# Keys turned by VectorE and transfers instead of TensorE, SyncE's program laid out by steps, and two small operations moved to ScalarE

## What is computed

```
Q, K = (x @ Wq.T), (x @ Wk.T)              # 16 heads of 64
V    = x @ Wv.T                            # 16 heads of 16
g    = -exp(A_log) * softplus(x @ Wdt.T + dt_bias);  cg = cumsum(g)
Lam  = softplus(Lp * (x @ Wdl.T))          # 12 levels for each head
W    = (Q K^T / 8) * exp(cg_t - cg_s) * Lam[t, level(t xor s)]    (s <= t)
a    = layernorm((W V) @ Wout.T + x) * ln_g + ln_b
x    = layernorm(x + a)                    # the "outer norm"
for two steps t:  f, i, u = sigmoid, sigmoid, tanh of (x_t @ w + c @ u + b);  c = f*c + i*u
x    = layernorm(x + tanh(x @ wo.T + c @ uo.T + bo))
```

## Time and profile before

| | |
|---|---|
| time, median of 3 runs | 681.56 us (680.77 to 683.13) |
| time of the profiled execution | 682.09 us |
| its span (first to last instruction) | 680.5 us |
| granted TensorE clock, mean | 0.982 of full speed |
| DMA engines, mean busy share | 25.6% for the kernel's own transfers |
| DMA packets under 512 bytes | 39664 of 91987 |

### The profile page before, as it was taken

How to read it: one execution, slowest core, us unless ns; L and a number is a source line. 1 busy time by engine, 2 the same in 40 slices (tenths; PEclk the granted TensorE clock), 3 DMA queues, 4 the chain that set the end, 5 groups by cost and what they waited for, 6 DMA issues and landing times.

```text
span 680.5 us, 22147 instructions
## 1 busy us (share of the span) xinstructions
PE 657.1 (97%) x9114; PEld 594.8 (87%) x9114; DVE 486.8 (72%) x1100; ACT 337.0 (50%) x755; POOL 353.9 (52%) x475
## 2 busy tenths in 40 slices
PE   9989999999999999999999999999689999999994
PEld 7889999999999999899999999999588788888894
DVE  2864887879787978676797879787749565555556
ACT  4565454445545454545445454545253434555555
POOL 1716555646474655656464646556365435444435
PEclk9999999999999999999999999999888999999997
DMA  8122131312222141213132322313126503140002
GB/s 306 30 56 60 48 75 41 76 46 71 64 53 76 42 94 42 64 41 76 43 74 55 60 73 45 87 50 82 53 71 122 103 9 62 47 86 31 32 33 92
DMA packets 91987, 45.47 MB, mean 67 GB/s; under 512 B 39664, under 2 KB 90480, under 8 KB 91888
## 3 DMA queue, kind: packets, MB, share of 16 engines
q1 hardware_dynamic: 91888, 44.06, 25.6%
HBM read 34.60 MB, written 9.44 MB: 65 GB/s over the span
## 4 chain that ended last, share of the span: by engine, by line
PE 86%; DVE 5%; ACT 2%; POOL 2%; DMA 1%; SPq 1%; issue 1%; DVEq 0%; ACTq 0%; POOLq 0%
PE bank L437 64%; PE bank L461 5%; PE bank L528 5%; PE bank L440 5%; PE bank L493 4%; PE bank L557 4%; DMA xt<-in_wffn 1%; ACT t L791 1%; SPq L371 1%; DVE t L1028 1%; DVE t L1031 1%; POOL t L1415 1%; SPq L348 0%; POOL yL L1415 0%; DVE W L1028 0%
## 5 line engine op out<-in xcount | busy, mean ns | idle before, releaser
L437 PE MATMUL bank<-xH,wH 128*128 128x256 f32 x480 | 144.3, 301 | 1.2 <-ACT KT L791 0.9
L437 PE MATMUL bank<-xL,wH 128*128 128x256 f32 x480 | 135.0, 281 | 0.0
L437 PE MATMUL bank<-xH,wL 128*128 128x256 f32 x480 | 134.6, 280 | 0.0
L1028 DVE TENSOR_TENSOR W<-bank,E 128x512 f32<-128x512 f32 x128 | 82.0, 685 | 25.7 <-PE bank L437 25.4
L437 PEld LDWEIGHTS bank<-xH,wH 128*128 128x128 f32 x480 | 90.4, 188 | 7.8 <-issue 7.3
L437 PEld LDWEIGHTS bank<-xL,wH 128*128 128x128 f32 x480 | 90.5, 189 | 0.4
L437 PEld LDWEIGHTS bank<-xH,wL 128*128 128x128 f32 x480 | 90.5, 188 | 0.0
L791 ACT ACTIVATE E<-bank 128x512 f32<-128x512 f32 x128 | 66.1, 602 | 48.8 <-PE bank L461 48.8
L791 ACT ACTIVATE QT<-bank 128x512 f32<-128x512 f32 x64 | 38.2, 597 | 98.5 <-PE bank L437 98.5
L437 PE MATMUL bank<-QT,KT 64*128 64x128 f32 x1024 | 65.8, 278 | 0.0
L437 PEld LDWEIGHTS bank<-QT,KT 64*128 64x128 f32 x1024 | 59.6, 188 | 4.5 <-issue 0.5
(11 more groups left out here) (151 smaller groups left out, 1657.9 us busy)
## 6 DMA issues: line engine op xcount, KB each, us to landing
cB<-scr SPq DMA_DIRECT2D x240, 64.0 KB, 3.0
xt<-in_xT SPq DMA_DIRECT2D x16, 256.0 KB, 3.1
xs<-in_x SPq DMA_DIRECT2D x16, 256.0 KB, 3.1
xscr<-tx SPq DMA_DIRECT2D x32, 128.0 KB, 2.0
yT<-xscr SPq DMA_DIRECT2D x64, 64.0 KB, 2.4
out<-xs SPq DMA_DIRECT2D x16, 256.0 KB, 2.1
xt<-in_wffn SPq DMA_DIRECT2D x8, 256.0 KB, 3.1
QT<-in_wqk SPq DMA_DIRECT2D x4, 256.0 KB, 5.7
```

What stands on the lines that cost most here:

```text
L437: return e.matmul(o, a, b, start=start, stop=stop)
L1028: return e.tensor_tensor(o, a, b, op)
```

## The change

- TensorE's `keys` and ScalarE's copies of them are gone. VectorE turns KT in blocks of 32x32 (`turn_keys`, four operations of 128x512 for a supergroup, q = 0 to 3), into a new tile `kx`. SyncE stores each of them to DRAM (`store_keys`, 256 KB), and for each chunk four transfers of 1024 pieces of 32 numbers bring Kt back with its blocks in their places (`load_keys`, 512 KB for a chunk). `state` waits for these transfers (`l_Kt`). For the first supergroup the tile W serves in place of kx.
- `key_jobs` puts q = 0, 1, 2, 3 of supergroup sg at steps 8sg-7, 8sg-4, 8sg-3 and 8sg, at the end of VectorE's step. Kt of the even chunk is loaded at step 8sg, after q = 3, and that of the odd chunk at 8sg+3, once `state` of the even chunk has read Kt.
- SyncE's list runs over the same steps as those of the other engines, and the loads of the cell's weights and of `xt` are placed by step.
- `outer_norm` is on ScalarE, in two operations (a negation of 128x1 and a scaled sum of 128x256), with one more of 128x1 on GpSimd; the residual is written into xs instead of x1. `turn_result` stands one step later, with one buffer tx instead of two.
- The copy of the decays (`cgt<-bank`, 128x320) is on ScalarE but for the first supergroup.

```diff
+def key_jobs(s):
+    out = []
+    for d, q in ((7, 0), (4, 1), (3, 2), (0, 3)):
+        if (s + d) % 8 == 0 and 1 <= (s + d) // 8 < NSG:
+            out.append(((s + d) // 8, q))
+    return out
...
-        if s % 4 == 0 and cc < CB - 1:
-            out += [("keys", ci, 0), ("keys", ci, 1)]
...
+            def store_keys(sg, q):
+                e.wait_ge(d_kx, 4 * sg + q + 1)
+                src, done = (kx[:, :], l_kx) if sg else (W[:, 4 * q:4 * q + 4, :].rearrange("p h t -> p (h t)"), l_k0)
+                e.dma_start(kscr[4 * sg:4 * sg + 4, :, 512 * q:512 * q + 512].rearrange("i t c -> (i t) c"),
+                            src).then_inc(done, 16)
+
+            def load_keys(ci):
+                sg, c = ci // 2, ci % 2
+                e.wait_ge(l_kx, 64 * sg) if sg else e.wait_ge(l_k0, 64)
+                if STATE[ci]:
+                    e.wait_ge(p_st, STATE[ci])
+                for j in range(4):
+                    b = 128 * c + 32 * j
+                    e.dma_start(Kt[32 * j:32 * j + 32, :].rearrange("t (q i f) -> t q i f", q=8, i=4),
+                                kscr[4 * sg:4 * sg + 4, :, :].rearrange("i t (q b) -> t q i b", q=8)[:, :, :, b:b + 32]
+                                ).then_inc(l_Kt, 16)
...
-            for sg in range(NSG):
-                if sg == NSG - 1:
-                    for i in range(2, 7):
-                        load_wf(i)
-                load_coefs(sg)
-                if sg == NSG - 1:
-                    load_turned(0, 1)
-                for ci in (2 * sg - 3, 2 * sg - 2):
-                    if ci >= 0:
-                        store_turned(ci)
-                if sg + 3 < NSG:
-                    e.wait_ge(g_xl, sg + 1)
-                    load_xt(sg + 3)
-                if sg + 2 < NSG:
-                    load_x(sg + 2)
-                if sg >= NSG - 3 and sg < NSG - 1:
-                    e.wait_ge(g_xl, sg + 1)
-                    load_wf(sg - NSG + 3)
...
+            for s in STEPS:
+                for i in [i for i in range(8) if s == (NG - 20 if i < 2 else NG - 17 + i)]:
+                    load_wf(i)
+                for sg, j in token_jobs(s):
+                    if j == 5:
+                        store_coefs(sg)
+                if (sg := split_x_at(s)) is not None and sg + 2 < NSG:
+                    e.wait_ge(g_xl, sg)
+                    load_xt(sg + 2)
+                if (ci := chunk_at(s, 12)) is not None:
+                    store_turned(ci)
+                for q in range(4) if s == -2 else ():
+                    store_keys(0, q)
+                for sg, q in key_jobs(s):
+                    store_keys(sg, q)
+                if 0 <= s < NG and s % 8 == 3 and s // 4 + 1 in STATE:
+                    load_keys(s // 4 + 1)
+                if 0 < s < NG and s % 8 == 0 or s == -1:
+                    load_keys(max(s, 0) // 4)
+                for sg, j in token_jobs(s):
+                    if j == 5:
+                        load_coefs(sg)
+                        if sg + 2 < NSG:
+                            load_x(sg + 2)
...
@@ TensorE, state
-                km, ku = MISC["keys", ci, 0]
-                e.wait_ge(m_free[km], ku + 1)
-                km, ku = MISC["keys", ci, 1]
-                e.wait_ge(m_free[km], ku + 1)
+                e.wait_ge(l_Kt, 64 * (STATE[ci] + 1))
...
@@ ScalarE
+            def outer_norm(ci):
+                e.wait_ge(g_rs2, ci + 1)
+                act(nb2[:, :], nm2[:, :], ACT.Copy, scale=-1.0).then_inc(a_n2, 1)
+                e.wait_ge(a_n2, ci + 1)
+                act(xs[:, ci, :], xs[:, ci, :], ACT.Identity, scale=rs2[:, 0:1], bias=nb2[:, 0:1]).then_inc(a_x2, 1)
...
@@ VectorE
+            def turn_keys(sg, q):
+                e.wait_ge(a_qk, 8 * sg + 2 * q + 2)
+                src = KT[sg % 2][:, 2 * q:2 * q + 2, :].rearrange("p m t -> p (m t)")
+                if sg == 0:
+                    o = W[:, 4 * q:4 * q + 4, :].rearrange("p h t -> p (h t)")
+                else:
+                    o = kx[:, :]
+                    if sg > 1 or q:
+                        e.wait_ge(l_kx, 16 * (4 * (sg - 1) + q))
+                e.transpose(o, src).then_inc(d_kx, 1)
...
-                if (ci := chunk_at(s, 11)) is not None:
-                    outer_norm(ci)
+                if (ci := chunk_at(s, 12)) is not None:
                     turn_result(ci)
+                for sg, q in key_jobs(s):
+                    turn_keys(sg, q)
```

More of the change, by code:

```diff
@@ L191, in program @@
         oo = sb("oo", [P, 256])
-        x1 = sb("x1", [P, 256])
-        tx = [sb(f"tx{i}", [P, 256]) for i in range(2)]
+        tx = sb("tx", [P, 256])
+        kx = sb("kx", [P, 512])
         st1 = sb("st1", [P, 6])
@@ L352, in store_turned @@
                 e.wait_ge(d_tx, ci + 1)
[L353 to L354 removed]
+                e.dma_start(xscr[4 * ci:4 * ci + 4, :, :].rearrange("i f c -> (i f) c"), tx[:, :]).then_inc(l_tx, 16)
+            def store_keys(sg, q):
[13 more added lines that the diff above has]
+                                ).then_inc(l_Kt, 16)
             def load_turned(blk, t):
                 c0 = 16 * t + 4 * blk
[L359 to L360 removed]
+                e.wait_ge(l_tx, 16 * (c0 + 4))
                 if blk == 0:
@@ L752, in _ @@
                 if 0 <= ci < NC:
-                    if n == 0 and ci in STATE:
-                        keys(ci)
                     if n == 1:
@@ L816, in project @@
                     e.wait_ge(p_sc, 4 * (sg - 2) + 4)
+                if sg >= 2 and j == 1:
+                    e.wait_ge(d_kx, 4 * (sg - 2) + 4)
                 if q:
@@ L842, in tokens @@
                     act(t4[:, :, :], t3[:, :, :], ACT.Exp, scale=-1.0).then_inc(a_lw, 1)
+                if j == 3 and sg:
+                    m, u = MISC["cgt", sg, 0]
+                    e.wait_ge(p_cg, sg + 1)
+                    e.wait_ge(d_ll, sg)
+                    e.wait_ge(g_at, 2 * sg)
+                    act(cgt[:, :], MB[m][:, 0:320], ACT.Copy).then_inc(m_free[m], 1)
                 if j == 8:
@@ L878, in exps @@
                     act(E[:, :, 32 * q:32 * q + 32], XP[q][:, :].rearrange("p (h t) -> p h t", h=H), ACT.Exp).then_inc(a_e, 1)
-            def keys(ci):
-                for n in range(2):
-                    m, u = MISC["keys", ci, n]
-                    e.wait_ge(p_kt, 2 * STATE[ci] + n + 1)
-                    if ci - 1 in STATE and n == 0:
-                        e.wait_ge(p_st, STATE[ci - 1] + 1)
-                    act(Kt[:, 512 * n:512 * n + 512], MB[m][:, :], ACT.Copy).then_inc(m_free[m], 1)
             def split_ffn(i):
@@ L990, in _ @@
                     act(c0H[:, :, :], bc(c0, 2, 2), ACT.Copy).then_inc(a_c0, 1)
-                if 0 <= s < NG and s % 4 == 0 and s // 4 in STATE:
-                    keys(s // 4)
                 for sg, j in project_jobs(s):
@@ L1003, in _ @@
                         tokens(sg, j)
+                if (ci := chunk_at(s, 11)) is not None:
+                    outer_norm(ci)
                 if s in SPLIT_AT:
@@ L1361, in _ @@
             for s in STEPS:
+                if s == -2:
+                    for q in range(4):
+                        turn_keys(0, q)
                 if (ci := chunk_at(s, 5)) is not None:
```

80 lines of the change are left out of this document (40 added, 40 removed).

## The result

The changed kernel takes 767.4 us (761.97 to 773.01); the kernel before took 682.4 beside it. The ratio is 1.125, with a 95% interval of 1.116 to 1.134. That is far above the forecast of 690 and above its range too (664 to 718). The profiled execution took 761.97 us, with a span of 759.8.

The account below looks back on a forecast made before the run. TensorE, 97% busy, was taken to bound the kernel. 682.1 - 30.6 + 44.8 + 1.2 + 0.6 - 9.5 + 1.5 = 690.1, against the median 689.6; likeliest 690, range 664 to 718.

Parts of the forecast that it names:

- Keys off TensorE: 30 groups of eight key transposes, 1.02 us each, leave TensorE's path: 30.6 us come off.
- the hole: Near the loop's end, TensorE's 7.68 us pause behind a late weight load, and slow groups after it, go: 9.5 us off.
- The 1.5 for the next weight loads: Later weight loads keep their buffer wait and stand among key transfers: 1.5 us given back, bounds 0 and 5.
- The chain to Kt: Tokens, softplus, `t3`, q = 3, store, load make even chunks' `state` wait: 14 x 3.2 = 44.8 us; half the chance.
- SyncE's list just in time: SyncE's cB transfers and x load end at 226.5, the next store is due at 227.7: 1.2 us to spare.
- The link to softplus: VectorE's `t3` starts at 224.82, having waited 0.57 us for GpSimd's softplus; the change leaves this alone.
- the clock as a rival: TensorE's clock falls after each even chunk's pause: 15 x 1.8 = 27 us more, 717; chance 0.2.
- Kt in time: Kt lands before `state` needs it and TensorE meets VectorE next: 664, or 644 were that hidden; chance 0.22.
- the bound named for it, VectorE's CT: With Kt on time, TensorE waits for VectorE's CT in the odd chunk: 1.4 us x 14 = 20.
- SyncE falls behind: Store, cB, Kt and x loads in one list block one another, cB or x late too: above 711, chance 0.08.
- The Trainium skill's rule: TensorE's clock is throttled after idle time and released by activity, so longer pauses are the ones at risk.

Follow-up runs that it names:

- the two kernels at 673.5 and 673.9: Changed kernel with keys back on TensorE: 673.51 us; kernel before with only SyncE's list by steps: 673.91 us.
- the reordered kernels: Changed kernel with q = 3 and its load ahead of half the cB transfers: 678.96 us; later also keys at both ends on TensorE, first yT loads earlier: 665.37.

## Why the prediction was wrong, point by point

- **Keys off TensorE, -30.6; the hole, -9.5.** Both right. The hole's is confirmed by the two kernels at 673.5 and 673.9, 8 to 10 us below the one before. The 1.5 for the next weight loads among the key transfers show in no wait of TensorE for ScalarE (0.8 for QT in all); one of these loads had a part in chunk 30's late store, below.
- **The chain to Kt.** Right in its links and in its place: even chunks only, q = 3 at 13 us after the tokens, SyncE's list just in time. Two terms were too small. The store landed after 2.55 us and, in the trace with q = 3 earlier, 3.55, against 2.3. The load took 6.6 against 5.3, above my upper bound of 6.1: I had counted the engines' time and a fixed 2.0, but the last of four transfers is issued after 2.4 us (3.24 less 0.8) and lands 3.9 after that. The landing was to be around 3 us each. Kt was so 1.5 us later than forecast, and the wait of chunk 12 still only 3.28 against 2.9, because TensorE itself came to `state` 1.2 us later (18.8 us after the tokens, forecast 17.65), in part by small waits for VectorE. The link to softplus was closer than I had it: around 266 VectorE's updates of the states end at 253.37 and softplus at 253.15, so `t3` waits for either as much. The waits of the 14 even chunks are 57.5 - 1.8 - 5.1 = 50.6, or 3.6 each against 3.2. Chunk 30 waited 5.1 against 1.2: VectorE had turned its q = 3 at 588.6, the store went out at 589.6 behind 16 cB transfers, a weight load and a store of the result, the load of Kt followed only 5.0 us later (594.6) and took 7.0.
- **The step that failed: the clock as a rival.** The forecast took the pause at full clock, and the falling clock as another case at 0.2. It isn't another case: a pause of the size that I forecast, 3.2 us, is the condition for it, and I had noted that such pauses lay between the 1.4 us that left the clock alone and the 7.7 that didn't. Between two such rows an even chance was the least to give. The price was low as well. I took 1.8 us from two groups; the third group and the projections behind them are slow too, and the rows around 266 add up to 3.3.
- **That rival's sum.** It said 717. To 762 are 45: 11 for longer pauses, 50.5 - 27 = 23.5 for the clock, 12 for the small waits less the 1.5 already counted. Those small waits, VectorE's and mostly of 0.2 to 0.5 us, stood in no term of mine.
- **Kt in time, 664.** Not what the change does, but what the reordered kernels do. The first gave 679 and the last 665; the bound named for it, VectorE's CT, is the one that shows, though at 4 to 6 us and not 20.
- **SyncE falls behind.** In the changed kernel only for chunk 30; in the trace with q = 3 one step earlier it does in the middle of the loop too (store at 257.03).
- **The Trainium skill's rule** on the clock ("TensorE: Matmul & The Clock Gate", Part 1) would have pointed the same way as the runs here: throttled after idle time, released by activity. I cited it and gave it a fifth.

## What to carry to other kernels

Where an engine that is 97% busy is made to wait for something, ask two things: how long it waits, and whether its clock survives. A pause of 3.6 us cost 3.6 and about 3 more, so unless a row of the trace shows the clock surviving a pause of that size, its fall belongs inside the forecast. When work is moved from the bound to a queue, draw up the queue's list for a whole period first. Against the same kernel with keys on TensorE, turning them by transfers cost 94 us in one order of VectorE's and SyncE's lists; in another, with the few chunks at both ends left out and the first yT loads moved forward, the kernel was 8 us faster.

## What the runs showed of the hardware

- A pause of TensorE of 3.3 to 3.7 us between full stretches brought the granted clock to 0.50 about when work began again, and the loss was about 3.3 us in the rows read; filling it with matmuls of no use gained 19 us over the kernel. Without any key traffic, pauses of 7 us cost 2.6 on top, those of mostly 2 to 3.4 us 1.6 on average. The length of one pause doesn't tell which: pauses of 1.25, 1.83 and 2.30 us had slow groups behind them, and pauses of 2.22, 2.71 and 2.99 us had none.
- A load of 512 KB in pieces of 128 bytes, as four transfers, took 6.6 us from first issue to the waiting matmul (7.5 in the reordered kernel), in rows of 4 KB 5.1; landing of one is 3.9 and 2.7 us. The issue of one takes 0.81 and 0.69 us (3.24 and 2.74 for four) with 1024 and 32 pieces, so the number of pieces hardly shows in it. From the issue of a key store of 256 KB to that of the load that waits for it, four places read here took 2.55, 3.55, 4.8 and 5.0 us.
